# The preparation of an attention kernel rebuilt: x in quarters, normalisation folded into the convolutions, patches copied chunk by chunk

## The reference

```python
x = x + _L0_conv_ref(_gn(x), ...)
x = x + _L1_conv_ref(_gn(x))
```

```python
embed_w = prelu(conv1x1(x, Wa, ba), aa)
match_in = prelu(conv1x1(x, W1, b1), a1)
raw_w = extract_patches(embed_w, kernel, s)
ref = x.reshape(B, C, H // s, s, W // s, s).mean(axis=(3, 5))
ref = prelu(conv1x1(ref, W2, b2), a2)
w = extract_patches(ref, k, 1)
norm = jnp.maximum(jnp.sqrt(jnp.sum(w * w, ...)), EPS)
wn = (w / norm).reshape(B, -1, C // 2 * k * k)
xp = extract_patches(match_in, k, 1).reshape(B, -1, C // 2 * k * k)
yi = jax.nn.softmax(einsum('blc,bqc->blq', wn, xp) * SOFTMAX_SCALE, axis=1)
yt = jax.vmap(tconv)(yi, raw_w)
yd = conv(yt, Wd, stride 2, pad 1) + bd
return yd / 6.0
```

## Time and profile before

| | us |
|---|---|
| median of 3 runs | 292.5 (291.15 to 293.56) |
| profiled execution | 292.99 |
| its span, first to last instruction | 291.2 |
| PE, PEld, DVE, ACT, POOL busy | 196.5, 177.5, 164.6, 145.8, 137.6 |
| mean granted TensorE clock | 0.833 of 2.4 GHz |

### The profile page before, as it was taken

The page is one execution under the profiler, slowest core; times in us unless marked ns, Lnnn a source line. Parts: engine busy times, 40 slices in busy tenths (PEclk is TensorE's granted clock), DMA queues, the critical chain, the costliest instruction groups (busy, mean ns, idle before and its releaser), DMA issues.

```text
span 291.2 us, 3619 instructions
## 1 busy us (share of the span) xinstructions
PE 196.5 (67%) x1162; PEld 177.5 (61%) x1162; DVE 164.6 (57%) x315; ACT 145.8 (50%) x273; POOL 137.6 (47%) x122
## 2 busy tenths in 40 slices
PE   0054753833735999479595989797959599965095
PEld 0032743732624998479494979696849498964083
DVE  2664133467365357666555567675977726756812
ACT  1257044875965656556558477657445222322030
POOL 8700106044433986219970977699446991000000
PEclk9999999965655779889879599897998859999555
DMA  7105985210110004961121000004011100000412
GB/s 194 19 0 76 101 114 150 81 42 0 22 34 1 2 0 43 118 103 50 33 83 40 0 0 2 0 2 80 3 41 44 40 0 2 0 0 2 98 25 41
DMA packets 10595, 12.30 MB, mean 42 GB/s; under 512 B 7888, under 2 KB 7888, under 8 KB 10096
## 3 DMA queue, kind: packets, MB, share of 16 engines
q1 hardware_dynamic: 10576, 12.07, 22.5%
HBM read 3.32 MB, written 1.18 MB: 15 GB/s over the span
## 4 chain that ended last, share of the span: by engine, by line
PE 36%; DVE 21%; ACT 13%; issue 11%; POOL 9%; SPq 5%; DMA 3%; DVEq 0%; POOLq 0%; ACTq 0%
PE zt L706 12%; PE yt L721 7%; PE ps L685 6%; POOL nt L526 4%; DVE negm L1087 3%; DVE bnst L970 3%; DVE nt L1104 3%; DVE v L1136 3%; DVE yl L1113 2%; ACT zneg L826 2%; PE pm L753 2%; SPq L386 2%; PE pd L733 2%; ACT z L828 2%; DMA v<-mimg 2%
## 5 line engine op out<-in xcount | busy, mean ns | idle before, releaser
L706 PE MATMUL zt<-ident,nt 128*125 128x128 f32 (+1 forms) x360 | 60.6, 314 | 21.9 <-DVE nt L1104 21.9
L706 PEld LDWEIGHTS zt<-ident,nt 128*125 128x125 f32 (+1 forms) x360 | 56.1, 212 | 24.9 <-issue 24.3
L526 POOL TENSOR_TENSOR nt<-nt 128x599 f32<-128x599 f32 (+1 forms) x42 | 56.8, 1353 | 27.0 <-ACT nt L892 17.9
L1113 DVE TENSOR_TENSOR yl<-zt,yh 125x384 fp32r<-125x384 f32 (+1 forms) x60 | 33.4, 557 | 36.1 <-ACT yh L900 21.9
L884 ACT ACTIVATE nt<-ps,negm 128x576 f32<-128x576 f32 x32 | 23.7, 742 | 48.9 <-DVE negm L1087 48.8
L900 ACT ACTIVATE yh<-zt 125x384 fp32r<-125x384 f32 (+1 forms) x60 | 29.1, 485 | 26.2 <-PE zt L706 25.7
L516 POOL TENSOR_TENSOR ml<-vim,mh 128x384 fp32r<-128x384 f32 x12 | 16.8, 1401 | 49.9 <-ACT mh L860 49.8
L892 ACT ACTIVATE nt<-nt,rps 128x599 f32<-128x599 f32 x36 | 28.6, 795 | 5.0 <-DVE rps L1094 4.6
L685 PE MATMUL ps<-wh,mh 128*128 128x288 f32 x64 | 19.7, 397 | 13.7 <-POOL mr L520 8.9
L1087 DVE TENSOR_REDUCE negm<-ps 128x1 f32<-128x576 f32 x32 | 24.1, 752 | 8.4 <-PE ps L685 8.2
L1136 DVE SCALAR_TENSOR_TENSOR v<-pd,v 32x384 f32<-32x384 f32 (+3 forms) x48 | 26.3, 547 | 2.8 <-PE pd L733 1.3
(11 more groups left out here) (126 smaller groups left out, 415.0 us busy)
## 6 DMA issues: line engine op xcount, KB each, us to landing
nt<-nt SPq DMA_DIRECT2D x12, 285.2 KB, 3.0
vim<-mimg SPq DMA_DIRECT2D x4, 432.0 KB, 8.3
xn<-x SPq DMA_DIRECT2D x6, 192.0 KB, 3.5
v<-mimg SPq DMA_DIRECT2D x6, 144.0 KB, 6.9
xn<-x SPq DMA_DIRECT2D x6, 96.0 KB, 2.6
v<-x SPq DMA_DIRECT2D x2, 288.0 KB, 4.5
vim<-mimg SPq DMA_DIRECT2D x2, 288.0 KB, 11.8
x_copy<-v SPq DMA_DIRECT2D x2, 288.0 KB, 2.8
```

The costliest lines, as they stand in the source:

```text
L526: pool.tensor_tensor(nt[:, dst, (to + 1) * KP + 1:(to + 1) * KP + 1 + n], nt[:, one, (row1 + 1) * KP + 1:(row1 + 1) * KP + 1 + n], nt[:, o ...
L706: last = nc.tensor.matmul(turned(zt[:, m % 2, :], n, col, TPC), keys_at(tile, r + dr, n, shift), ident[:, :], start=at == 0, stop=at == le ...
L1113: nc.vector.tensor_tensor(yl[0:n, m % YBUF, :].rearrange("p (h j) -> p h j", j=W), turned(zt[:, m % 2, :], n), F(yh[0:n, m % YBUF, :]).rea ...
```

## The change

x is loaded once per image, in four transfers: a quarter of the rows on each group of 32 partitions. The statistics are taken by quarter and joined by one small matmul. x itself is not normalised; the inverse root scales the weights of the three convolutions (`weights`), and the mean goes into their biases through six one-column matmuls (`biases`). The half-size image is added up on POOL (`pooled`). Each convolution is computed quarter by quarter on 32 rows, with three products (high-high, low-high, high-low): conv1 in eight pieces of 288 columns, conv2 and the embedding in pieces of 144 columns, with a wait between row groups (`other_rows`). For even pieces DVE takes the negative part itself from PSUM, for odd ones ACT does. conv1 writes its image in row blocks with neighbours doubled, so that the patches of one chunk are contiguous; they are copied chunk by chunk, six transfers each, and each chunk's split waits for its own. The squares are taken from the image and not from the patches (ACT two row groups, POOL one), and `norm` has 18 matmuls. The embedding of image 0 (`emb`, `ek`) moves from `BEFORE` into steps 1 to 3; the jobs of image 1 shift, its convolutions to steps 8 to 12, its embedding to steps 15 and 16. The output weights are loaded and split later. POOL does `two_columns` ahead of the row sums of the same step. Parameters are loaded by ACT's queue.

```diff
+    ("xs", (0,)), ("mean", (0,)), ("low", (0,)), ("weights", (0,)), ("bias", (0,)), ("conv2", (0, 1)),
+    ("conv1", (0, 1)), ("squares", (0,)), ("conv1", (2, 3, 4)), ("norm", (0,)), ("conv1", (5, 6, 7)),
+    ("inorm", (0, 1)), ("keys", (0,)), ("split", (0, 1))]
...
-    ("residual", 0, 1, 4, 1), ("rows", 1, 3, 7, 1.5), ("scale", 1, 2, 12, 1), ("low", 1, 2, 13, 1),
-    ("conv2", 1, 2, 16, 1), ("conv1", 1, NCH, 19, 1), ("squares", 1, 1, 28, 1), ("norm", 1, 1, 30, 1),
-    ("inorm", 1, 2, 33, 1), ("keys", 1, 1, 37, 1), ("emb", 1, 2, 39, 1), ("ek", 1, 2, 41, 2), ("residual", 1, 1, 60, 1),
+    ("emb", 0, 2, 4, 2), ("ek", 0, 2, 9, 2), ("xs", 1, 1, 13, 1), ("mean", 1, 1, 15, 1), ("low", 1, 1, 17, 1),
+    ("weights", 1, 1, 20, 1), ("bias", 1, 1, 23, 1), ("residual", 0, 1, 28, 1), ("conv2", 1, 2, 26, 1),
+    ("conv1", 1, 8, 29, 1), ("squares", 1, 1, 33, 1), ("norm", 1, 1, 35, 1), ("inorm", 1, 2, 38, 1),
+    ("keys", 1, 1, 41, 1), ("emb", 1, 2, 46, 2), ("ek", 1, 2, 51, 2), ("residual", 1, 1, 60, 1),
...
-                for part, arrived in ((slice(0, X_FIRST), s_x0[b]), (slice(X_FIRST, Q), s_x[b])):
-                    for r in range(3):
-                        sp.dma_start(xn[C * r:C * (r + 1), part], src[:, part]).then_inc(arrived, 16)
-
-            def im2col(b, image, ready, row, size, full, last, done):
-
-                sp.wait_ge(s_const, 6)
-                sp.wait_ge(ready, 1)
+                for r in range(4):
+                    sp.dma_start(x4[b][C * r:C * (r + 1), :],
+                                 src[:, QUARTER * r:QUARTER * (r + 1)]).then_inc(s_x4[b], 16)
...
+            def match_patches(b):
+
+                sp.wait_ge(s_const, 6)
+                sp.wait_ge(s_mimg[b], 1)
+                for t in range(NCH):
+                    if b:
+                        sp.wait_ge(s_split, NCH * (b - 1) + t + 1)
+                    im2col(mimg, 1 + CHUNK * t, CHUNK, CHUNK, vim, v2, slice(CHUNK * t, CHUNK * (t + 1)), s_mim[t])
...
+            load_x(0)
+            ref_patches(0)
+            match_patches(0)
+            sp.dma_start(x1(0), x[0].rearrange("c h w -> c (h w)")).then_inc(s_xin[0], 16)
+            load_x(1)
+            output_weights()
+            sp.dma_start(cosm[:, :], dct).then_inc(s_cos, 16)
+            sp.dma_start(x1(1), x[1].rearrange("c h w -> c (h w)")).then_inc(s_xin[1], 16)
+            move_up(0)
+            ref_patches(1)
+            match_patches(1)
...
+            first = before.index(("low", 0, 0))
             perform(before[:first], handlers)
+            zeros()
+            pool.wait_ge(s_tiles, NTILE_EDGES)
+            perform(before[first:], handlers)
             output_weights()
-            perform(before[first:], handlers)
             for s in range(steps):
+                if s >= 8 and s % TPC == 2 and (s - 8) // TPC < NG:
+                    two_columns((s - 8) // TPC)
                 if s < NT:
                     row_sums(s // TPC, s % TPC)
                 row_sums_over_edge(s)
-                if s >= 8 and s % TPC == 2 and (s - 8) // TPC < NG:
...
+            def conv(o, q, at, width, xh, xl):
+
+                rows = slice(C * q, C * (q + 1))
+                for n, (w, v) in enumerate(((wsh, xh), (wsh, xl), (wsl, xh))):
+                    last = nc.tensor.matmul(o, w[rows, at:at + width], v, start=n == 0, stop=n == 2)
+                return last
...
+                q, cols = i // 2, slice(HALF * (i % 2), HALF * (i % 2 + 1))
+                rows = slice(C * q, C * (q + 1))
+                conv(o[0:96, 0:HALF], q, S_W1, 96, x4h[rows, cols], x4l[rows, cols]).then_inc(s_mf, 1)
...
+                for k in range(2):
+                    q = 2 * i + k
+                    rows = slice(C * q, C * (q + 1))
+                    if k:
+                        other_rows(last)
+                    dst = o[:, REFQ * k:REFQ * (k + 1)]
+                    parts = [v[rows, :].rearrange("p (i u j v) -> p i u j v", u=2, j=WL, v=2) for v in (x4h, x4l)]
+                    for n in range(4):
+                        at = S_WA + C * (3 - n)
+                        for m, (w, v) in enumerate(((wsh, 0), (wsh, 1), (wsl, 0))):
+                            last = nc.tensor.matmul(dst, w[rows, at:at + 128], parts[v][:, :, n // 2, :, n % 2],
+                                                    start=n + m == 0, stop=n == 3 and m == 2)
...
+                    for r in range(3):
+                        at = WL * r + 96 * n + 1
+                        last = nc.tensor.matmul(o[0:96, n:n + 1], sq[:, at:at + 96], ones[0:96, 0:1], start=r == 0,
+                                                stop=r == 2)
...
+                if k % 2:
+                    nc.scalar.activation(zneg[0:rows, 1, :], o[0:rows, 0:HALF], ACT.Relu,
+                                         bias=nbias[0:rows, which:which + 1], scale=-1.0)
+                nc.scalar.activation(z[0:rows, k % 2, :], o[0:rows, 0:HALF], ACT.Relu,
+                                     bias=bias[0:rows, which:which + 1]).then_inc(s_z, 1)
...
+                root = gm[b][:, 3:4]
+                two = slice(S_W2, S_W2 + 96)
+                link(nc.vector.tensor_scalar_mul(wsf[:, two], par[:, P_W2:P_W2 + 96], root))
+                link(nc.vector.tensor_copy(wsh[:, two], wsf[:, two]))
+                nc.vector.tensor_tensor(wsl[:, two], wsf[:, two], F(wsh[:, two]), ALU.subtract).then_inc(s_w2[b], 1)
...
+            def prelu(name, b, i, rows, which, dst, *more):
+
+                k = convs.index((name, b, i))
+                o = group(dve, name, b, i)
+                slope = par[0:rows, P_A1 + which:P_A1 + which + 1]
+                dve.wait_ge(s_z, k + 1)
+                if k % 2:
+                    slope = nslope[0:rows, which:which + 1]
+                else:
+                    link(nc.vector.tensor_scalar(zneg[0:rows, 0, :], o[0:rows, 0:HALF], bias[0:rows, which:which + 1], 0.0,
+                                                 ALU.add, ALU.min))
+                for to, part in more:
+                    link(nc.vector.scalar_tensor_tensor(out=to, in0=part(zneg[0:rows, k % 2, :]), scalar=slope,
+                                                        in1=part(z[0:rows, k % 2, :]), op0=ALU.mult, op1=ALU.add))
+                wide = list(dst.shape)[-1]
+                nc.vector.scalar_tensor_tensor(out=dst, in0=zneg[0:rows, k % 2, :].rearrange("p (h w) -> p h w", w=wide),
+                                               scalar=slope, in1=z[0:rows, k % 2, :].rearrange("p (h w) -> p h w", w=wide),
+                                               op0=ALU.mult, op1=ALU.add).then_inc(s_free["dve"], 1)
...
```

446 lines of the change are left out of this document (247 added, 199 removed).

## The result

The changed kernel takes 333.35 us (median, 331.72 to 334.88) against 292.51 of the kernel before in the same session: 1.140 times as long, 95% interval 1.132 to 1.147. Forecast were 298.5 us and a range up to 307. The sign was right, the size was not: 41 us instead of 6.

What follows compares the result with a forecast made beforehand. No engine carried the whole chain; PE was the bound from tile 9 on. Tile 9 -3.0, tiles 9 to 18 +10.5, POOL's order -1.0 made +6.5, less 0.5: +6, 298.5 us, range 286 to 307.

Steps and rivals of the forecast that it cites:

- Tiles 9 to 18: Stretch taking in image 1's first convolution, norm and dearer embedding: 10.5 us longer in all.
- steps 9 to 11: Image 1's conv1 pieces arrive, with PE, ACT and DVE nearly equally loaded: 24 us, +7.
- Steps 12 to 14: They lose the embedding and its waits: from 20.05 us to 15, -5.
- Steps 15 to 17: They take both halves of image 1's embedding in line, and its transposes: +8.5 us.
- The start: Up to the first exp: image ready 7.1 us later, but chunk-wise patch copy brings the exp 4.9 us earlier.
- The wait on POOL: POOL stands until output weights land at 66.4 us; tile 6 comes at 72.0, leaving 0.4 of the 4.9 us.
- Tile 9: Its row maximum comes at 86 us against 89.02, the stretch behind tile 6 being lighter: -3.0 us.
- two_columns first: POOL adds two columns before the last row sums, so DVE waits less: -1.0 us.
- The slow rival: DVE's two-input passes are slowed beside POOL between tiles 9 and 18: 8 us more, 306.5 us; chance 0.15.
- Rival 1: Added pieces fill idle time of PE and ACT: 290.5 us, down to 287; chance 0.25.

Runs made afterwards that it cites:

- bare_norm: The changed kernel without two of the three shifted sums of the keys' norm, 12 of 18 matmuls for each image: 325.5 us.
- emb1_late: The changed kernel with the embedding of image 1 moved from steps 15 and 16 to 20 and 22, its turn to 24 and 25: 321.3 us.
- weights_early: The changed kernel with SP's loads of the output weights moved up behind load_x(0): 328.5 us.
- two_last: The changed kernel with POOL's old order, row sums ahead of the sum of two columns: 331.5 us.
- chunks_keys: The kernel before with the chunk-wise image in eight pieces, 36 chunk-wise transfers, keys and first queries' parts ahead of the embedding, its turn in step 0: 296.5 us.

## Why the prediction was wrong

- **Tiles 9 to 18, "together +10.5 us"**, is the step that failed; it measured +31.1. Its three parts: steps 9 to 11 were forecast at 24 us and took 25.9, which is near. **Steps 12 to 14, "20.05 to 15, -5"**, took 28.0: I let the embedding go out of them and forgot what came in. The norm of image 1 was priced only as "+1.1" of PE's work; it stands in order ahead of the scores of tile 13, unhidden, with the last pieces of the convolution before it. 13 us off. From tile 12 to 13 the norm is 5.89 us of the way (bare_norm won 3.8 there with two thirds of it gone), and a piece with its two waits 3.4. **Steps 15 to 17, "+8.5"**, took +14.0: 0.155 us a matmul would be 3.7 us for 24; it took 5.7 (0.21 apart, at the lower clock level) and 3.9, and the products behind went at the lower level too (0.32 us apart at 168 instead of 0.17 at 179 in emb1_late). The forecast priced the matmuls of these steps at the upper level; how much of the 31 us the lower one is, no run tells.
- **The start, "-4.9 us"**: measured -0.5. The norm's size was right (6.2 forecast, 5.9 measured), and so was its place; what failed stands ahead of the biases, done at 17.0 instead of 12.9, 4.1 of the 5.1 us by which the image is late against the forecast. POOL's zeroing of tiles runs beside the weight steps: 1.05 and 1.08 us for two of the size that takes 0.16 in the earlier trace rows make 1.8 of the 4.1; 2.43 us for two casts holds what is behind them. Another 1.0 is there before the weight steps begin (9.6 instead of 8.6). And the six bias matmuls took 2.5 us (12.86 to 15.36): the forecast had 1.5, though the row it named says 2.08. From the biases to the norm it took 9.7 us where I had 9.5. The last three pieces behind the norm took 1.2 more than I had.
- **The wait on POOL** was right in kind and price: output weights in at 70.9 (66.4), tile 6 at 76.5 (72.0), both late by about what the image was late. That the embedding of image 0 costs nothing under this wait and shows when it goes was right too: weights_early took the wait away and won 0.6 us at tile 6.
- **Tile 9, "-3.0"**: +4.2, of which 4.5 is tile 6; from 6 to 9 it took 16.7 us where I had 14, no less than before.
- **two_columns first, "-1.0"**: +4.4 us in the kernel before, 3.4 of them behind tile 18. In the changed kernel its price isn't shown: two_last won 3.3 us behind tile 18 and lost 3.6 ahead of it. The forecast had the wrong sign: I looked at whom DVE waits for and not at whom POOL's pass slows.
- **The rivals.** The slow rival named a right mechanism (passes beside POOL: 1.74 us instead of 0.52) at 8 us; in the changed kernel's trace 6 of 44 passes into the image were slowed, by 4.3 us together, all between tiles 9 and 15. No rival was that a block in TensorE's order stops the scores, and order and place made some 31 us. Rival 1, that pieces fill holes, is refuted: ACT waited 27.5 us for the maxima in the stretch, so there were holes, and the pieces as placed did not use them.
- **The two pages of the Trainium skill.** SP's transfer from image to patches took a median of 0.592 us (36 of them), so the trace stays at twelve times the 50 ns of the Trainium skill, DMA: Bandwidth & Descriptors, § Where the ~2 µs actually goes; the page gives them for a transfer on GpSimd's path, and these were SP's. With the rule of the Trainium skill, TensorE: Matmul & The Clock Gate, § LDWEIGHTS, the trace agrees: weight loads of 32 rows (L736) took 267 to 272 ns in the mean, those of 128 rows (L783) 251 to 266, both between tiles 9 and 18.

## What to carry to other kernels

On an engine that takes its instructions in order, price a side job by what stands behind it: here the same embedding cost 12.7 us in one step and 3.6 in another (the granted clock changed with it), and two pieces in a step with two banks cost less than three. When a wait is taken away, look at the tile that it held: if that tile hardly moves, something else was waiting underneath. When work is moved, make two lists for each stretch, what leaves and what arrives, and let each thing that arrives stand ahead of the next scores until a cover for it is named. A stretch in which no engine is full isn't a stretch with room.

## What the runs showed of the hardware

- The norm's one-column fp32 matmuls took 0.164 us a record at the start, where the granted clock reads 1.00, and in the loop, where it is 0.50: 5.89 us both times. The twelve of the kernel before took 2.08 us at 28 us, and 1.10 in chunks_keys at 103 us, where the granted clock reads 1.00 and scores had just gone at the upper level. So the matmuls of the start go at the lower of the two levels (1.2 GHz) although the granted clock reads 1.00 there.
- DVE's steps on SBUF alone can be slowed beside POOL, also beside its memsets: 0.16 to 1.05 us for three columns, 0.52 to 1.74 for 96x288 with two inputs, 0.27 up to 1.23 for 96x48. DVE's passes with an operand in PSUM took the same in all stretches (L1149 0.51, L1259 0.56). The slow pass at 106.38 ended at 108.12, 0.3 us behind the two POOL sums that ran from 105.00 to 107.80. The Trainium skill, SBUF — State Buffer, § SBUF: two separate sides, says that a VectorE step with two inputs in SBUF and a GpSimd step that reads SBUF need the same pair of ports, and that the one that starts first has it for its whole instruction. The trace agrees here.
